# Expert rows gathered by number, results added in memory by accumulating DMAs, expert weights split inside the batch loop

## The chip, the cores and the metric

The kernel runs on one core of one Trainium2 chip. The metric is the device time of one execution in microseconds (us). Before the change three runs gave 1304.9, 1306.76 and 1310.32 us, a median of 1306.76.

The engines: PE (TensorE, the matmuls; PEld is its weight load), DVE (VectorE), ACT (ScalarE), POOL (GpSimd) and SP (SyncE, which here only issues DMAs). ACT and POOL issue DMAs too. POOL alone issues the indirect ones, in which a list of row numbers says which row of a tensor in memory each partition reads or writes. Every engine takes its instructions in order; a wait in front of one holds back all that stand behind it on that engine.

## What is computed

x is (16, 256, 512): 16 batches of 256 tokens of width 512. Cut to what matters:

```
x2   = x + tanh(g_xattn) * mlstm(layernorm(x), ctx, ctx)          # 8 heads of 64, causal decay matrix
n    = layernorm(x2)                                              # 4096 tokens x 512
top2 = top_k(softmax(n @ router_w.T), 2); w = top2 / sum(top2)    # of 16 experts
y    = sum over the 2 chosen experts e of  w_e * (silu(n @ gate_e) * (n @ up_e)) @ down_e    # 512 -> 256 -> 512
s    = (silu(n @ shared_gate) * (n @ shared_up)) @ shared_down    # 512 -> 512 -> 512
out  = x2 + tanh(g_ffn) * (y + s)
```

Each token goes to two experts, so 8192 rows are routed. An expert's weights are 128 partitions x 3072 numbers (1.5 MB). To keep fp32 accuracy each matmul of the second half is done in three parts, with a high and a low part of weights and activations (hi*hi, hi*lo, lo*hi); the weights are therefore "split" into a high part (a cast) and a low part (the rest), 3 MB together.

## The kernel before

**Batch loop.** 16 batches in a software pipeline: step t runs the front of batch t+1 (transposes of x and context, gate rows), the attention of batch t (eight `head`s), the first part of the feed-forward of batch t-1 (layer norm `post_norm` L1353 to L1356, transposes, `router`, shared parts 0 and 1) and the rest of batch t-2 (shared parts 2 and 3, `shared_down`, `rank`). Each engine has this order written out by hand in its own `step`; semaphores tie them together. POOL's `scatter` (L495) writes each normalized row twice, by four indirect DMAs a batch (L501), to `routed_x`, sorted by expert. DVE keeps base rows (x2 + shared part) of all 16 batches in `base_out`, and the routing in `all_hot`, `all_slot`, `all_w`. The shared weights are split at the start by two long POOL instructions (L527, L530) and fill the whole of `w_ring`, which later holds two experts.

**Between.** After the last batch (`drain`) DVE makes tables: how many rows each expert has, where each tile of 128 rows starts, which expert it belongs to. The rest of each expert's last tile is filled with zero rows (`pad_rows`; 17 writes of 256 KB). Expert 0 is split by ACT (L817) and DVE (L1597), expert 1 by POOL (L601, L604).

**Expert stage.** 80 tiles of 128 rows. SP loads tile t (L394, 256 KB) into a ring of four. PE transposes it (`turn_rows` L1125), ACT and DVE make its high and low part, PE multiplies by gate and up (`gate_up` L1137, 12 matmuls), ACT and DVE make the activation (L826, L1603, L1607), PE transposes it (L1146), DVE makes its parts (L1614, L1616), PE multiplies by down (L1155, 6 matmuls). ACT copies the result out (`copy_y` L832) and stores it to `routed_y` (L837). Meanwhile POOL splits the expert after next (L618, L621) and loads one more (L485). PE's order in a tile is: transposes of tile t+2, activation transposes of tile t, gate and up of t+1, down of t.

**Combine.** When all 80 results are stored, POOL gathers for each of 32 token tiles the two result rows of each token (L641, two indirect DMAs of 256 KB), DVE weights and adds them (L1661, L1666), SP stores 256 KB to the output (L423).

## Time and profile before

| what | us |
|---|---|
| median of three timed runs | 1306.76 (1304.9 to 1310.32) |
| span of the profiled execution, first to last instruction | 1302.3 |
| median less span | 4.5 |
| batch loop and drain, up to the last shared matmul | about 794 |
| first expert matmul (L1137) | at 803.98 |
| last result tile stored (L837 issued) | at 1203.90 |
| combine, from there to the end | 98.4 |

The profiled execution has no time of its own beside its span; the 4.5 us is the distance of the span to the median of the other runs. PE is busy 84% of the span, DVE 64%, POOL 38%, ACT 29%. PE is busy in nine tenths or more of nearly every slice from 65 to 715 us and from 830 to 1200 us. In the views, times are from the start of the span; a share in square brackets at a line's end is the idle time before an instruction and what ended it.

### The profile page before, as it was taken

How to read it: one execution, taken by the hardware profiler on the slowest of the kernel's cores; microseconds unless marked ns; L12 is line 12 of the kernel's file. 1: busy time of each engine (PE TensorE's matmuls, PEld its weight loads, DVE VectorE, ACT ScalarE, POOL GpSimd, SP SyncE). 2: the span in 40 equal slices, each digit the busy share in tenths (PEclk: the TensorE clock that was granted, in tenths of full speed). 3: DMA queues.
4: the chain of work that ended last, by engine and by line, in shares of the span. 5: the costliest groups of instructions: out<-in, count | busy, mean ns of one | idle time of the engine just before them, and what ended most of it. 6: DMA issues, size and time to landing. Idle time of an engine off the chain costs nothing.

```text
span 1302.3 us, 24291 instructions
## 1 busy us (share of the span) xinstructions
PE 1098.4 (84%) x6611; PEld 910.9 (70%) x6612; DVE 827.1 (64%) x2212; ACT 371.4 (29%) x820; POOL 491.8 (38%) x368
## 2 busy tenths in 40 slices
PE   2289999999999999999999765999999999999000
PEld 1167888878788887788788664788888888887000
DVE  3756878888788788788877644544444444444455
ACT  1133233424333333343333102223233232232000
POOL 3600222222222222222212335356656566700775
PEclk9666999999999999999999778999999999999555
DMA  5000001110111011001000244555464645321787
GB/s 205 32 33 33 33 34 66 57 42 32 65 57 41 33 65 65 17 32 49 33 1 34 82 172 156 175 181 176 158 205 149 209 151 187 128 98 64 239 283 260
DMA packets 57869, 134.53 MB, mean 103 GB/s; under 512 B 7088, under 2 KB 7088, under 8 KB 57808
## 3 DMA queue, kind: packets, MB, share of 16 engines
q0 software_dynamic: 17472, 59.78, 14.0%
q1 hardware_dynamic: 26128, 48.51, 11.2%
q10 hardware_dynamic: 14208, 25.57, 5.5%
q8 instruction: 22, 0.36, 0.1%
q14 instruction: 39, 0.32, 0.1%
HBM read 83.23 MB, written 50.59 MB: 103 GB/s over the span
## 4 chain that ended last, share of the span: by engine, by line
PE 72%; DVE 12%; issue 7%; DMA 5%; ACT 2%; POOL 0%; DVEq 0%; ACTq 0%; POOLq 0%
PE bank L1137 18%; PE bank L1001 10%; PE bank L1155 9%; PE bank L1012 7%; PE bank L937 5%; PE bank L913 5%; DMA area<-routed_y,y_at 4%; PE bank L879 3%; PE bank L1125 3%; PE bank L942 2%; PE bank L954 2%; PE bank L939 2%; PE bank L955 2%; PE bank L957 2%; PE bank L1146 1%
## 5 line engine op out<-in xcount | busy, mean ns | idle before, releaser
L1137 PE MATMUL bank<-w_ring,x2nT 128*128 x960 | 246.0, 405 | 8.6 <-DVE w_ring L1597 8.6
L1137 PEld LDWEIGHTS bank<-w_ring,x2nT 128*128 128x128 f32 x960 | 175.3, 189 | 48.9 <-issue 10.0
L1001 PE MATMUL bank<-x2nT,w_ring 128*128 128x256 f32 x1536 | 200.2, 288 | 7.8 <-DVE sh_act L1434 7.8
L1001 PEld LDWEIGHTS bank<-x2nT,w_ring 128*128 128x128 f32 x1536 | 190.2, 194 | 9.2 <-DVE sh_act L1434 5.4
L501 POOL DMA_INDIRECT routed_x<-x2n,slot_u x64 | 67.5, 1054 | 192.9 <-DVE slot_u L1424 178.3
L1288 DVE SCALAR_TENSOR_TENSOR area<-bank,area 128x384 f32<-128x384 f32 x128 | 71.4, 557 | 96.7 <-ACT area L712 61.4
L1155 PE MATMUL bank<-w_ring,sh_actT 128*128 x480 | 125.2, 396 | 2.1 <-DVE sh_actT L1616 2.1
L1603 DVE SCALAR_TENSOR_TENSOR ctxT<-ctxT,bank 128x256 f32<-128x256 f32 x80 | 33.7, 421 | 142.7 <-ACT ctxT L826 142.7
L710 ACT ACTIVATE area<-bank,key_log 128x256 f32<-128x256 f32 x128 | 60.7, 474 | 212.1 <-PE bank L944 176.2
L522 POOL TENSOR_TENSOR sh_actT<-sh_act,sh_actT 128x256 fp32r<-128x256 f32 x64 | 54.5, 852 | 167.9 <-ACT sh_actT L727 167.8
L618 POOL TENSOR_TENSOR w_ring<-area,one 128x3072 fp32r<-128x3072 f32 x14 | 74.3, 5304 | 114.4 <-PE bank L1155 114.4
L1155 PEld LDWEIGHTS bank<-w_ring,sh_actT 128*128 128x128 f32 x480 | 90.0, 188 | 24.4 <-issue 2.8
L1012 PE MATMUL bank<-w_ring,sh_actT 128*128 128x512 f32 x384 | 102.5, 412 | 2.3 <-DVE sh_act L1434 1.4
L641 POOL DMA_INDIRECT area<-routed_y,y_at x64 | 67.4, 1053 | 87.1 <-DMA routed_y<-cs_in 67.9
L621 POOL TENSOR_TENSOR w_ring<-area,w_ring 128x3072 fp32r<-128x3072 f32 x14 | 95.6, 6831 | 2.5 <-POOL w_ring L618 2.5
L937 PE MATMUL bank<-area,ctxT 64*128 64x256 f32 x256 | 94.7, 452 | 1.8 <-issue 1.5
L826 ACT ACTIVATE ctxT<-bank 128x256 f32<-128x256 f32 x80 | 30.8, 384 | 204.6 <-PE bank L1137 204.6
L1012 PEld LDWEIGHTS bank<-w_ring,sh_actT 128*128 128x128 f32 x384 | 70.4, 193 | 22.0 <-POOL sh_actT L522 5.4
L1614 DVE CAST sh_actT<-bank 128x256 fp32r<-128x256 f32 x80 | 34.0, 425 | 63.6 <-PE bank L1146 63.3
L832 ACT COPY cs_in<-bank 128x512 f32<-128x512 f32 x80 | 46.9, 587 | 87.2 <-PE bank L1155 87.2
L939 PEld LDWEIGHTS bank<-area,ctxT 64*128 64x128 f32 x256 | 51.1, 200 | 8.8
L937 PEld LDWEIGHTS bank<-area,ctxT 64*128 64x128 f32 x256 | 39.9, 195 | 23.5 <-issue 15.7
(203 smaller groups left out, 2059.0 us busy)
## 6 DMA issues: line engine op xcount, KB each, us to landing
x2n<-routed_x SPq DMA_DIRECT2D x80, 256.0 KB, 2.8
routed_y<-cs_in ACTq DMA_DIRECT2D x80, 256.0 KB, 2.1
base_out<-in_x_dram SPq DMA_DIRECT2D x16, 512.0 KB, 4.4
cs_in<-in_ctx_dram SPq DMA_DIRECT2D x16, 512.0 KB, 3.7
area<-n_L_ffn_expert_gate_dram POOLq DMA_DIRECT2D x16, 512.0 KB, 4.1
area<-in_L_ffn_expert_up_dram POOLq DMA_DIRECT2D x16, 512.0 KB, 4.9
area<-n_L_ffn_expert_down_dram POOLq DMA_DIRECT2D x16, 512.0 KB, 6.9
out_dram<-area SPq DMA_DIRECT2D x32, 256.0 KB, 4.2
```

What stands on the lines that cost most here:

```text
L501: pool.indirect_dma_start(out=routed_x, in_=x2n[:, b.par, j, :], in_offset=None, out_offset=bass.IndirectOffsetOnAxis(ap=slot_u[:, b.par, ...
L618: g.tensor_tensor(w_ring[:, k, 0, :], stage[k], one[:, :].to_broadcast([P, EW]), ALU.mult).then_inc(expert_hi_in.sem, 1)
L621: g.tensor_tensor(w_ring[:, k, 1, :], stage[k], w_ring[:, k, 0, :], ALU.subtract).then_inc(expert_in.sem, 1)
L641: pool.indirect_dma_start(out=y_in[k][:, c, :], in_=routed_y, out_offset=None, in_offset=bass.IndirectOffsetOnAxis(ap=y_at[:, k, c:c + 1], ...
L913: last = mm(SM[0:FG + NH, 0:S], gate_wT[:, c, :], src, start=(c == 0), stop=(c == 2 * DC - 1))
L937: mm(QK[k][:, 0:S], ctxT[rows, b.par, c, 0:P], xnT[rows, b.par, c, 0:S], start=True, stop=True)
L939: mm(QK[k][:, S:TRI], ctxT[rows, b.par, c, P:S], xnT[rows, b.par, c, P:S], start=True, stop=True).then_inc(qk_made.sem, 1)
L1001: last = mm(GU[m][:, at:at + S], w[:, w_part, c, m * P:(m + 1) * P], x2nT[:, x_part, c, :], start=(c + p == 0), stop=(c == DC - 1 and p == 2))
L1012: last = mm(FF[:, :], sh_actT[:, x_part, m, j * P:(j + 1) * P], sh_down[:, w_part, m, :], start=(m + p == 0), stop=(m == SC - 1 and p == 2))
L1137: last = mm(bank[2 + t.par][:, :], xtT[:, x_part, t.par, c * P:(c + 1) * P], w_gu[:, bass.ds(slot, 1), w_part, c, :].rearrange("p a i -> p ...
L1155: last = mm(bank[5 + t.par][:, :], act_aT[:, x_part, t.par, c * P:(c + 1) * P], w_dn[:, bass.ds(slot, 1), w_part, c, :].rearrange("p a i - ...
L1288: v.scalar_tensor_tensor(cmat[:, k, :], QK[k][:, 0:TRI], QK_SCALE, decay[:, k, :], ALU.mult, ALU.mult).then_inc(c_made.sem, 1)
```

## The change

- **Rows go by number.** The normalized rows are stored once, in token order, to `normed` (SP, 512 KB a batch). What is scattered by expert is 8 bytes a row, token number and weight (`meta` to `routed`), still four indirect DMAs a batch. In the expert stage ACT loads the 128 pairs of tile t+4 (`load_meta`, a register load from a table and a DMA), and POOL gathers the tile's rows from `normed` by number.
- **Results are added in memory.** The base rows are stored to `total` (SP, 512 KB a batch). `copy_y` multiplies by the weight, and POOL adds the tile's 128 rows to `total` by an indirect DMA that accumulates (`scatter_y`). It waits for the accumulation of the tile before (`y_added`). ACT waits for the one of tile t-4 before it goes on to `load_meta` and `tanh_gate` of tile t+1. Then eight DMAs of 1 MB, from memory to memory, copy `total` to the output. The combine is gone.
- **Experts are split early.** In step t of the batch loop expert t+1 (in the last, expert 0) is split in six pieces of 128x512: SP loads a piece, ACT casts the high part, POOL subtracts for the low part, SP stores both to `split_w` (512 KB). In the expert stage SP loads one whole split expert (3 MB) by one DMA into a ring of three.
- The split of the shared weights is six POOL instructions of 2048 columns in place of two of 6144. PE's instructions are the same ones in the same order.

The diff, cut to its core:

```
-RING = 2
+RING = 3
 @block.sync
+            def next_piece(t, k, e, e_next):
+                sp.wait_ge(piece_lo.sem, piece_lo.upto(t.n, k + 1))
+                if e is not None:
+                    sp.dma_start(split_w[...piece k of e...], split[:, :, k * PIECE:(k + 1) * PIECE].bitcast(F32)
+                                 ).then_inc(piece_out[k].sem, 16)
+                if k < RAW:
+                    load_piece(e_next if e is None else e, k + RAW)
+                elif e_next is not None:
+                    load_piece(e_next, k - RAW)
...
+            load_expert(1)
+            load_expert(2)
+            told(1)
+            for e in range(3, E):
+                used = sp.value_load(first_tab[0:1, e - 2:e - 1], min_val=0, max_val=TILES)
+                sp.wait_ge(y_made.sem, used + y_made.start)
+                load_expert(e)
+                told(e - 1)
+            told(E - 1)
+            sp.wait_ge(y_added.sem, y_added.upto(TILES - 1))
+            for k in range(HALVES):
+                sp.dma_start(out_tok[k * COPY:(k + 1) * COPY, :], total[k * COPY:(k + 1) * COPY, :]
+                             ).then_inc(copied[0].sem, 16)
 @block.gpsimd
+            def piece(t, k):
+                pool.wait_ge(piece_hi.sem, piece_hi.upto(t.n, k + 1))
+                g.tensor_tensor(split[:, 1, at], raw[:, k % RAW, :], split[:, 0, at], ALU.subtract
+                                ).then_inc(piece_lo.sem, 1)
...
+            def gather(t):
+                pool.wait_ge(meta_in[t.eight].sem, meta_in[t.eight].upto(t.lap8))
+                pool.wait_ge(xt_turned.sem, xt_turned.upto(t.n - XRING))
+                pool.indirect_dma_start(out=xt[:, t.four, :], in_=normed, in_offset=tile_meta[:, t.eight, 0:1])
+            def scatter_y(t):
+                pool.wait_ge(y_copied.sem, y_copied.upto(t.n))
+                pool.wait_ge(y_added.sem, y_added.upto(t.n - 1))
+                pool.indirect_dma_start(out=total, in_=y_out[:, t.four, :], out_offset=tile_meta[:, t.eight, 0:1],
+                                        compute_op=ALU.add).then_inc(y_added.sem, 16)
...
 @block.scalar
+            def piece(t, k):
+                act.wait_ge(raw_in[k % RAW].sem, raw_in[k % RAW].upto(t.n * 2 + k // RAW))
+                act.wait_ge(piece_out[k].sem, piece_out[k].upto(t.n - 1))
+                s.copy(split[:, 0, k * PIECE:(k + 1) * PIECE], raw[:, k % RAW, :]).then_inc(piece_hi.sem, 1)
...
             def copy_y(t):
                 act.wait_ge(y_made.sem, y_made.upto(t.n))
-                s.copy(y_out[:, t.par, :], bank[5 + t.par][:, :]).then_inc(y_copied.sem, 1)
+                s.activation(y_out[:, t.four, :], bank[5 + t.par][:, :], ACT.Copy,
+                             scale=tile_meta[:, t.eight, 1:2]).then_inc(y_copied.sem, 1)
+            def expert_step(t, fill=False, ahead4=True, ahead2=True, ahead1=True):
                 if ahead2:
                     copy_x(t + 2)
+                if not fill:
+                    act.wait_ge(y_added.sem, y_added.upto(t.n - YRING))
+                if ahead4:
+                    load_meta(t + XRING)
                 if ahead1:
                     tanh_gate(t + 1)
                 copy_y(t)
 @block.vector
-            v.tensor_tensor(w_ring[:, 0, 1, :], stage[0], w_ring[:, 0, 0, :], ALU.subtract
-                            ).then_inc(expert_in.sem, 1)
...
-            then(v.tensor_tensor(hot_shift, hot, shift[:, :].unsqueeze(1).to_broadcast([P, B * ST * TOPK, E]),
-                                 ALU.mult))
-            then(v.tensor_reduce(y_slot_f[:, :], hot_shift, AX_X, ALU.add))
```

Where POOL stands at the end of a step of the batch loop, before. The names: `area<-cs_in` copies the values of the next batch, the indirect DMAs are `scatter`, the last row is `keep` of shared part 0:

```order
L508 TENSOR_TENSOR x_rstd<-x_var,minus_half 128x2
L489 ISA
L491 COPY area<-cs_in 128x16x64
L501 DMA routed_x<-x2n,slot_u 67712x512 x4
L520 ISA
L522 TENSOR_TENSOR sh_actT<-sh_act,sh_actT 128x256
```

and now (`w_ring<-raw,w_ring` is the subtraction of a piece):

```order
L616 TENSOR_TENSOR x_rstd<-x_var,minus_half 128x2
L595 ISA
L597 COPY area<-cs_in 128x16x64
L652 REGISTER_ALU
L655 TENSOR_TENSOR w_ring<-raw,w_ring 128x512
L604 ISA
L609 DMA routed<-meta,slot_u 67712x2 x4
L652 REGISTER_ALU
L655 TENSOR_TENSOR w_ring<-raw,w_ring 128x512
L628 ISA
L630 TENSOR_TENSOR sh_actT<-sh_act,sh_actT 128x256
L652 REGISTER_ALU
```

Three of a step's six subtractions (pieces 3, 4 and 5) stand in this part: behind the copy of the values, behind the scatters and behind `keep`.

ACT in the same part of a step, before: the exponentials of head 5 and 6 (`area<-bank`), each with a copy of the transposed rows behind it (`x2nT<-bank`):

```order
L710 ACTIVATE area<-bank,key_log 128x256
L712 ACTIVATE area<-bank,key_log 128x128
L688 ISA
L676 CAST x2nT<-bank 128x4x128
L707 REGISTER_ALU
L710 ACTIVATE area<-bank,key_log 128x256
L712 ACTIVATE area<-bank,key_log 128x128
L688 REGISTER_ALU
L676 CAST x2nT<-bank 128x4x128
```

and now:

```order
L828 ACTIVATE area<-bank,key_log 128x256
L830 ACTIVATE area<-bank,key_log 128x128
L856 CAST w_ring<-raw 128x512
L806 ISA
L794 CAST x2nT<-bank 128x4x128
L825 REGISTER_ALU
L828 ACTIVATE area<-bank,key_log 128x256
L830 ACTIVATE area<-bank,key_log 128x128
L856 CAST w_ring<-raw 128x512
```

The cast of a piece now stands between the exponentials and the copy that PE's next transposes wait for.

POOL in the expert stage, before, one of the experts of a lap (a load of its table entry, the two halves of the split, the loads of a later expert):

```order
L613 TENSOR_LOAD first_tab
L613 ISA x2
L614 REGISTER_ALU
L618 TENSOR_TENSOR w_ring<-area,one 128x3072
L621 TENSOR_TENSOR w_ring<-area,w_ring 128x3072
L485 ISA
L485 DMA area<-in_L_ffn_expert_gate_dram 128x4x256
L485 DMA area<-in_L_ffn_expert_up_dram 128x4x256
L485 DMA area<-in_L_ffn_expert_down_dram 128x2x512
```

and now, two tiles (`x2n<-normed` gathers the rows of a tile, `total<-cs_in` adds its results):

```order
L731 REGISTER_ALU
L733 DMA x2n<-normed,tile_meta 128x512
L743 ISA
L745 DMA total<-cs_in,tile_meta 4224x512
L731 REGISTER_ALU
L733 DMA x2n<-normed,tile_meta 128x512
L743 ISA
L745 DMA total<-cs_in,tile_meta 4224x512
```

POOL has no arithmetic there any more, and two indirect DMAs a tile: 160 in all, the second of each pair behind the wait for the accumulation before it.

## Rows read from the trace of the kernel before

**Rows 1.** Page, part 2: busy tenths in 40 slices of 32.6 us.
```profile
PE   2289999999999999999999765999999999999000
DMA  5000001110111011001000244555464645321787
```
**Rows 2.** Page, part 4: shares of the chain that ended last.
```profile
PE 72%; DVE 12%; issue 7%; DMA 5%; ACT 2%; POOL 0%; DVEq 0%; ACTq 0%; POOLq 0%
```
**Rows 3.** Windows: PE, PEld, DVE, ACT, POOL busy, PE clock, DMA share, GB/s.
```profile
400.00:440.00 40.00, 39.03 (x278) 32.90 (x278) 31.55 (x97) 14.78 (x35) 10.24 (x11) 1.00 0.15 53
1000.00:1050.00 50.00, 50.00 (x245) 40.84 (x244) 23.39 (x51) 14.60 (x30) 34.12 (x12) 1.00 0.54 173
```
**Rows 4.** Timeline (start, us, instruction), before the first head.
```profile
42.12 13.17 POOL L530 TENSOR_TENSOR w_ring<-base_out,w_ring 128x6144 fp32r<-128x6144 f32 x1
44.59 10.97 DVE L1249 SCALAR_TENSOR_TENSOR f_row<-gates,f_row 8x256 f32<-8x256 f32 x1 [2.28 <-ACT f_row L697]
```
**Rows 5.** Page, part 5: POOL's subtraction for one expert.
```profile
L621 POOL TENSOR_TENSOR w_ring<-area,w_ring 128x3072 fp32r<-128x3072 f32 x14 | 95.6, 6831 | 2.5 <-POOL w_ring L618 2.5
```
**Rows 6.** Timeline, one step of the batch loop and the next step's first scatter.
```profile
421.83 0.58 ACT L676 CAST x2nT<-bank 128x512 fp32r<-128x512 f32 x1
422.50 0.68 DVE L1440 TENSOR_TENSOR x2nT<-bank,x2nT 128x512 fp32r<-128x512 f32 x1
423.30 0.61 PE L879 MATMUL bank<-ident,x2n 128*128 128x128 f32 x4
427.35 1.06 POOL L501 DMA_INDIRECT routed_x<-x2n,slot_u  x1 [11.84 <-DVE slot_u L1424]
431.25 1.39 POOL L501 DMA_INDIRECT routed_x<-x2n,slot_u  x1 [0.30 <-issue]
435.30 0.28 PE L925 MATMUL bank<-ident,key_max_rest 40*128 40x40 f32 x2 [0.61 <-issue]
471.03 1.06 POOL L501 DMA_INDIRECT routed_x<-x2n,slot_u  x1 [11.94 <-DVE slot_u L1424]
```
**Rows 7.** Chain of waits, from the batch loop into the expert stage.
```profile
795.29 7.82 DVE w_ring L1597
803.98 4.60 PE bank L1137 x12
819.56 0.10 DVE shift L1637
823.17 0.44 DVE sh_actT L1614
826.67 2.79 PE bank L1137 x12
```
**Rows 8.** Timeline at the same place, POOL and PE.
```profile
788.09 0.74 POOL L522 TENSOR_TENSOR sh_actT<-sh_act,sh_actT 128x256 fp32r<-128x256 f32 x1 [3.77 <-ACT sh_actT L727]
794.34 1.03 PE L1125 MATMUL bank<-ident,x2n 128*128 128x128 f32 x8
```
**Rows 9.** Chain of waits: gate matmuls of tile 79, last `copy_y`.
```profile
1195.57 2.98 PE bank L1137 x12
1203.21 0.59 ACT cs_in L832
```
**Rows 10.** Line L501 (indirect store): ns to issue; DMA, issue to landing.
```profile
L501 POOL DMA_INDIRECT routed_x<-x2n,slot_u x64: 956/962/1389, 169.8 to 769.7; - x64
DMA to landing us min/median/max: 2.7/2.8/3.9
```
**Rows 11.** Line L641 (indirect gather), issue to landing.
```profile
DMA to landing us min/median/max: 3.4/4.8/5.9
```
**Rows 12.** Line L837 (plain store of 256 KB), issue to landing.
```profile
DMA to landing us min/median/max: 2.0/2.1/7.5
```
**Rows 13.** DMA view: 895 to 925 us (40 slices), then 1206 to 1300 us.
```profile
GB/s 0 0 295 281 123 0 76 311 361 279 268 104 161 396 415 415 366 240 90 14 0 79 298 240 82 0 0 0 227 232 240 0 49 164 426 361 350 238 224 410
...
DMA packets 9585, 24.92 MB, mean 265 GB/s; under 512 B 1520, under 2 KB 1520, under 8 KB 9584
```

More of the change, by code:

```diff
@@ L76, in __add__, with __init__ @@
         return Item(self.i, self.offset + k)
+class Tile:
+    def __init__(self, i, offset):
+        self.i, self.offset = i, offset
+        self.n = i * 8 + offset
+        self.half = i * 4 + offset // 2
+        self.lap4 = i * 2 + offset // 4
+        self.lap8 = i + offset // 8
+        self.par, self.four, self.eight = offset % 2, offset % 4, offset % 8
+    def __add__(self, k):
+        return Tile(self.i, self.offset + k)
 def flamingo_kernel(nc, x, ctx_in, g_xattn, g_ffn, igate_w, igate_b, fgate_w, fgate_b, ln_scale,
@@ new lines, in step @@
+            def step(t, more=True, x_more=True, pieces=True, first=False, last=False, route=True, rest=True):
+                C, G, H = t + 3, t + -1, t + -2
+                e = None if last else t.n + 1
+                e_next = None if last else (0 if first == "end" else t.n + 2)
+                if pieces:
+                    for k in range(3):
+                        next_piece(t, k, e, 0 if last else e_next)
+                if more:
+                    sp.wait_ge(ctxT_made.sem, ctxT_made.upto(t.n + 1))
+                    apart(sp)
+                    sp.wait_ge(v_made.sem, v_made.upto(t.n + 1))
+                    apart(sp)
+                    load_ctx(C)
+                if x_more:
+                    sp.wait_ge(x_in[C.par].sem, x_in[C.par].upto(C.half - 1))
+                    apart(sp)
+                    if not isinstance(C.n, int) or C.n >= BASE:
+                        sp.wait_ge(base_stored[C.par].sem, base_stored[C.par].upto(C.half - BASE // 2))
+                        apart(sp)
+                    load_x(C)
+                if pieces:
+                    next_piece(t, 3, e, e_next)
+                if route:
+                    store_normed(G)
+                if pieces:
+                    next_piece(t, 4, e, e_next)
+                if rest:
+                    store_base(H)
+                if pieces:
+                    next_piece(t, 5, e, e_next)
@@ L399, in _ @@
-            with sp.Fori(0, E // 2) as e:
-                row = sp.value_load(pad_tab[0:1, bass.ds(e, 1)], min_val=0, max_val=DUMP - P)
-                sp.dma_start(routed_x[bass.ds(row, P), :], zeros[:, :]).then_inc(padded.sem, 16)
-            sp.dma_start(routed_x[DUMP:DUMP + P, :], zeros[:, :]).then_inc(padded.sem, 16)
+            for k in range(RAW):
+                load_piece(1, k)
+            step(Item(0, -1), x_more=False, pieces=False, route=False, rest=False)
+            step(Item(0, 0), x_more=False, route=False, rest=False)
@@ new lines, in _ @@
+            sp.wait_ge(shared_in.sem, shared_in.upto(2))
+            step(Item(0, 1), rest=False)
+            for n in range(2, 5):
+                step(Item(0, n))
+            with sp.Fori(0, (B - 8) // 2) as i:
+                for u in range(2):
+                    step(Item(i, 5 + u))
+            step(Item(0, B - 3), more=False, x_more=False)
+            step(Item(0, B - 2), more=False, x_more=False, first="end")
+            step(Item(0, B - 1), more=False, x_more=False, last=True)
@@ new lines, in scatter_y @@
+            def scatter_y(t):
+                pool.wait_ge(y_copied.sem, y_copied.upto(t.n))
+                apart(pool)
+                if not (isinstance(t.n, int) and t.n < 1):
+                    pool.wait_ge(y_added.sem, y_added.upto(t.n - 1))
+                    apart(pool)
+                pool.indirect_dma_start(
+                    out=total, in_=y_out[:, t.four, :], in_offset=None,
+                    out_offset=bass.IndirectOffsetOnAxis(ap=tile_meta[:, t.eight, 0:1].bitcast(U32), axis=0),
+                    compute_op=ALU.add,
+                ).then_inc(y_added.sem, 16)
@@ L654, in _ @@
+            for n in range(TILES - 8, TILES):
+                if n + XRING < TILES:
+                    gather(Tile(0, n + XRING))
+                scatter_y(Tile(0, n))
         @block.scalar
```

404 lines of the change are left out of this document (200 added, 204 removed).

## The prediction

> **What bounds the kernel now.** I read the 40 slices first [rows 1]. PE is full in two stretches, and in neither does DMA matter much (0 to 6 tenths). At the end there are three slices in which PE does nothing while the DMA engines are busy at 7 to 8 tenths: the combine. Between the stretches PE dips for three slices. The chain of waits says the same: 72% of it is PE, 12% DVE, 5% DMA [rows 2]. The windows give the slack of the others [rows 3]. In 40 us of the batch loop PE works 39.03, DVE 31.55, ACT 14.78, POOL 10.24; in 50 us of the expert stage PE works all 50, DVE and ACT under half, and the DMA engines are busy 0.54 of the time. So a step of the batch loop (43.7 us, from one batch's scatter to the next [rows 6]) and a tile each cost what PE needs, and a change there can only cost. A tile takes (1195.57 - 826.67) / 76 = 4.85 us, from the gate matmuls of tile 3 to those of tile 79 [rows 7, 9].
>
> What can be won is the combine and the passage from the batch loop to the experts. The question is what the new work does to the two full stretches.
>
> **Tail: -60.** Before, the last result is in SBUF at 1203.8 [rows 9] and the span ends at 1302.3, so 98.5 us. All of that goes. In its place: the last accumulation (4.2, see below), 0.5 for the issue, and 8.39 MB copied from memory to memory. No row shows such a copy. The combine moved 24.92 MB at 265 GB/s in the mean, rows of 2 KB read and written [rows 13]; at that rate 8.39 MB take 31.7 us. The best slice shows 426 GB/s [rows 13]: 19.7 us. If reading and writing memory shared the 265, it would be 63 us. I take 31.7, the nearest row (the mix of reads and writes is the same), and 2.0 for landing as in a plain store [rows 12]. Sum 38.4, gain 60.1. Bounds: 26 to 70, so a gain of 72 to 29.
>
> **Passage: -11.** The last shared matmul and the first transposes end at 795.4; then PE waits for DVE to split expert 0 (7.82 us) and starts at 803.98 [rows 7, 8]. Now expert 0 is split in the last step of the loop. What is late next is the first tile: POOL's gathers stand behind its last `keep`, which ends at 788.83 [rows 8]. The first, issued at 788.9, lands 3.4 later [rows 11] at 792.3, the second 1.3 behind, both before 794.3. Then cast and subtraction of the transposed tile, and PE starts at about 796.4: 7.6 us earlier. The number pairs come before that, at about 785, since the pads are 1 KB each and not 256 KB. Second, DVE no longer computes where each result row lies (L1637 to L1645, 819.56 to 823.17), for which PE waited: 3.6 us [rows 7]. Sum 11.2. If the gathers come late by one landing under load the gain is 7; it can't be above 13. The split of the shared weights has the same columns on POOL, and I cost its six parts at nothing: DVE's row chain now waits for four short instructions in turn where it waited once for 10.97 us [rows 4]; either way it is free when POOL is done. Bounds -4 to +3.
>
> **Batch loop: +20.** Each step gets six casts on ACT (0.58 each, the cast of 128x512 in [rows 6]), six subtractions on POOL (6.831 / 6 = 1.14 each [rows 5]) and about 20 DMA issues on SP, which has nothing else to do (two loads a step before). Stores and loads of pieces are 4.5 MB a step over 43.7 us, or 100 GB/s on engines that are busy 0.15 of the time [rows 3]: hidden, each load has some 10 us before its cast. The sums of ACT (14.8 + 3.5) and POOL (10.2 + 6.8) fit too. What isn't hidden is where they stand. (a) DVE stalls while POOL reads two tensors: an instruction of 8x256 that takes 0.41 us took 10.97 beside POOL's long one, until that ended [rows 4]. Piece 4 follows the scatters, whose last issue ends at 432.64, just when DVE makes the rows on which the logits and then PE's L925 wait; PE already stands 0.61 there [rows 6]. So one subtraction, 1.1 us, falls on the path. (b) The cast of piece 4 stands between the exponentials of head 5 and the copy of the transposed rows. The low part is ready at 423.18, PE uses it at 423.30 [rows 6]: of 0.58 some 0.45 falls on the path. The other pieces meet an idle ACT or have more than 1 us of slack. 1.55 a step, times 13 full steps: 20. Low bound 0 (DVE has 8 us idle in 40). High bound: half of all subtractions on the path, 3.5 a step: 46.
>
> The Trainium skill, "SBUF — State Buffer", section "SBUF: two separate sides", has it that the port pair of VectorE and GpSimd is an exclusive lock for the whole instruction, against DVE operations with two SBUF inputs or in a 2-port mode. By that rule each of the six pieces can stall DVE by up to its full length, and the step could lose 6.8 us where DVE is the last to be ready; the trace's 10.97 us agrees with the lock, and its DVE idle time speaks for less.
>
> **Expert stage: +31.** The tile's own work is unchanged. SP, ACT and DVE stay under half load. Two things are new: a chain of accumulations, each of which waits for the one before, and 3.1 MB an expert in one DMA where 1.5 MB was loaded. Call u the period of the chain on quiet DMA engines. A plain indirect store of 128 rows lands 2.8 after its issue starts, and POOL needs 0.3 to go on [rows 6, 10]: u can't be under 3.1. An accumulation also reads its target. If that read came wholly before the store it would be 3.4 + 2.8 + 0.3 = 6.5 [rows 11]. A gather, which has that read, takes 0.6 more than a store; I add about as much again for the doubled bytes and the longer descriptor list: u = 4.2, nearer to the lower row. The gather of another tile (1.25 of issue) lies in the flight of an accumulation. On top, a transfer that meets a loaded engine takes up to 7.5 for 2.1, that is 5.4 more [rows 12], and 3.1 MB at 350 to 426 GB/s [rows 13] occupy the engines for 8 us, so each expert's load meets one accumulation. With 80 / 16 = 5 tiles an expert: chain 5 x 4.2 + 5.4 = 26.4, PE 5 x 4.85 = 24.3. The chain is longer by 2.1, and ACT's wait for tile t-4 hands this on: behind it stand `load_meta`, `tanh_gate` and with it PE's down. The four buffers take up a burst, not a mean. 15 experts with loads: 31. Bounds: 0 (u = 3.1), and 15 x (37.9 - 24.3) = 204 (u = 6.5).
>
> **Sum.** 1302.3 - 60 - 11 + 20 + 31 = 1282; with the 4.5 by which the median stands over the span, 1287.
>
> On the accumulation the Trainium skill, "Collectives: The Full Stack", section "The bandwidth ceiling: the fold count and why AG ≠ RS ≠ AR", says that an add in the DMA engine costs no time of its own but a second read on the same ring. By that rule u would be a store and the doubled bytes; 256 KB at 426 GB/s are 0.6 us, so u = 3.7 and the sum 1256 (rival 1). No row of this case shows an accumulation.
>
> **Rivals.**
> 1. *The chain is hidden.* The second read costs only its bytes, u = 3.7 or less: 5 x 3.7 + 5.4 = 23.9, under PE's 24.3. For it: of a store's 2.8 only 0.96 is issue [rows 10], the rest can hold a read beside it; and 4.8 was the median of gathers on engines at eight tenths [rows 1, 11]. Against it: read, then write of memory is a path that neither has. Time: 1287 - 31 = 1256.
> 2. *The chain decides the stage, and the kernel is slower.* One mechanism: u at 5.5, because the target is read, added and written one after the other. Then 5 x 5.5 + 5.4 = 32.9 an expert, 8.6 over PE, 129 in all: 1287 + 98 = 1385. It turns the sign when the stage loses over 51, which is 3.4 an expert, from u = 4.5 on. For it: 4.5 is only 0.3 above my value, and the wait is strictly serial. Against it: only the upper bound of the rows reaches that far.
> 3. *The batch loop pays.* Pieces stop DVE or ACT on PE's path at 3.5 us a step: +46 in place of +20, 1313, no change. For it: DVE is at eight tenths there [rows 3]. Against: ACT and POOL have over half their time free.
>
> **How the numbers follow.** Forecast 0.37 (own range 1265 to 1302), rival 1 0.27, rival 2 0.27, rival 3 0.09. The likeliest is 1287. 0.5% of the median is 6.5 us, about what can be told from no change: 1300.2 to 1313.3 is "same". Faster: nearly all of the forecast and all of rival 1, less what a slow copy takes, 0.58. Slower: rival 2 from u = 4.54 and the bad half of rival 3, 0.32. Same: 0.10. The range reaches down to rival 1 with a quicker copy (1256 - 12, and a part of the batch loop's 20): 1240; up to rival 2: 1385. Where signs differ this much, the forecast's own 1265 to 1302 says more.
>
> **What would show it.** Steps: PE's last wait before the first gate matmul is for the tile, not for DVE, at about 816 (796 + 20). Batch steps are 45.2 us apart, L925's wait grows from 0.6 to about 1.7. Accumulations land about 4 us after issue, about 9 when an expert is loading; ACT waits for y_added in some tiles of each expert. A tile takes 5.2 in the mean. The copy takes 32. I am wrong if tiles stay at 4.85 (rival 1), if POOL waits for the accumulation before every tile and tiles take over 5.5 (rival 2), or if steps are 47 us or more (rival 3).

## The result: slower by 11%, and the profile after

Before 1308.54 us (1304.9 to 1310.51), after 1447.71 us (1445.75 to 1448.41). The ratio is 1.1065 with a 95% interval of 1.1035 to 1.1095. The forecast was 1287, its range ended at 1385: wrong in sign and out of range. The profiled execution after has a span of 1444.1 us against 1302.3, so 141.8 more, and it divides into the four terms of the sum without a rest:

| stretch, in the two traces | predicted | measured |
|---|---|---|
| batch loop (to the end of the last shared matmul: 794.34 to 847.86) | +20 | +53.5 |
| passage (from there to the first gate matmul: 9.64 to 2.15) | -7.6 | -7.5 |
| expert stage (first gate matmul to the moment at which the last result can go out: 399.8 to 560.1) | +31 - 3.6 | +160.3 |
| tail (98.5 to 34.0) | -60 | -64.5 |

Before, the last result can go out when it is in SBUF, at 1203.8. After, it is there at 1403.4 but has to wait until the accumulation of tile 78 has landed, at 1410.1.

The page after, part 2: busy tenths of PE, granted clock of PE, and DMA, in 40 slices of 36.1 us.

```profile
PE   3389999999999999999999576777777777779870
PEclk9568999999999999999999798888999999989995
DMA  5243453444444353434331166666666666765548
```

The three idle slices of [rows 1] are one now. But from slice 24 to 36 PE is mostly at seven tenths where it had nine. Its clock, 1.00 in [rows 3], is below full in both long stretches (0.93 and 0.90 in the windows below). Part 4 of the page, the chain that ended last, against [rows 2]:

```profile
PE 39%; DMA 33%; issue 11%; DVE 11%; ACT 2%; ACTq 1%; POOLq 0%; DVEq 0%; POOL 0%
DMA total<-cs_in,tile_meta 30%; PE bank L1135 9%; PE bank L1146 7%; PE bank L1071 5%; PE bank L1047 4%; PE bank L1076 2%; PE bank L1088 2%; DVE area L1462 2%; PE bank L1073 2%; PE bank L1013 2%; PE bank L1091 2%; PE bank L1089 1%; PE bank L
```

PE had 72% of the chain, now 39%. 30% of the span is one kind of transfer, the accumulation. Windows of the same places as [rows 3], then of the whole stage:

```profile
165.00:650.00 485.00, 458.00 (x3026) 387.40 (x3025) 399.86 (x1081) 193.24 (x435) 200.32 (x185) 0.93 0.44 144
850.00:1410.00 560.00, 431.38 (x1912) 337.88 (x1912) 182.06 (x399) 129.28 (x238) 201.02 (x155) 0.90 0.63 158
```

**The chain of accumulations.** The chain of waits in the middle of the stage (start, length, what):

```profile
1089.40 11.79 DMA total<-cs_in,tile_meta
...
1102.03 4.66 DMA total<-cs_in,tile_meta
...
1107.53 5.03 DMA total<-cs_in,tile_meta
...
1112.60 0.58 issue
...
1113.39 5.07 DMA total<-cs_in,tile_meta
...
1119.30 5.08 DMA total<-cs_in,tile_meta
...
1125.32 11.58 DMA total<-cs_in,tile_meta
```

Start to start the quiet period is 5.3 to 6.1 us nearly always, 5.8 in the mean: 4.6 to 5.1 in flight and 0.8 to 0.9 until POOL starts the next issue. Where a 3 MB load sets out at the same moment it is 12.6 in the mean. That is the arithmetic of the stage. From the start of the first accumulation (867.5) to that of the last (1410.9) there are 79 periods: 66 x 5.76 + 13 x 12.56 = 543.4. (Two of the 15 loads set out before the first accumulation, so 13 meet one. The text of e5_meta has 64 periods of 5.9 and 15 of 12.6; that comes near 560 only because it also leaves out the start.) The other 17.5 us lie between the first gate matmul and the first accumulation, and they hold a wait of the same kind: the small load of tile 4's numbers, issued beside the two first 3 MB loads:

```profile
854.21 11.05 DMA tile_meta<-routed
```

The groups of the accumulation (L745) and of the expert's load (L509), from issue to landing:

```profile
L745 POOL DMA_INDIRECT total<-cs_in,tile_meta x80: 1549/1592/1638, 867.5 to 1410.9; - x80
DMA to landing us min/median/max: 4.5/4.9/13.3
...
DMA to landing us min/median/max: 10.6/11.1/18.9
```

An accumulation takes 1.59 us to issue against 0.96 of the plain indirect store [rows 10], and lands after 4.9 against 2.8.

**The batch loop.** Timeline of the end of one step (start, length, instruction, idle time before):

```profile
549.95 1.88 DVE L1400 CAST max_parts<-max_row 8x256 bf16<-8x256 f32 x1
550.37 1.30 POOL L655 TENSOR_TENSOR w_ring<-raw,w_ring 128x512 fp32r<-128x512 f32 x1
554.40 0.29 PE L1059 MATMUL bank<-ident,key_max_rest 40*128 40x40 f32 x2 [2.09 <-issue]
557.62 5.13 PE L1135 MATMUL bank<-x2nT,w_ring 128*128 128x256 f32 x24
```

DVE's cast (8x256, 0.28 us at the shortest in this trace) stands until POOL's subtraction of piece 4 is over, and PE's wait, 0.61 in [rows 6], is 2.09. The prediction had both. What it did not have is the last row: the 24 shared matmuls, which take 3.05 us elsewhere in the step, take 5.13. The windows around it show the clock:

```profile
552.00:558.00 6.00, 3.81 (x21) 3.00 (x20) 4.46 (x16) 0.93 (x4) 1.94 (x2) 0.78 0.63 218
558.00:564.00 6.00, 6.00 (x34) 5.68 (x34) 2.85 (x8) 1.90 (x5) 2.70 (x3) 0.65 0.55 186
564.00:570.00 6.00, 6.00 (x52) 5.68 (x51) 5.16 (x11) 3.20 (x8) 3.33 (x3) 1.00 0.49 157
```

After the wait of 2 us the granted clock is at its lower level, 1.2 GHz, for 6.8 us (555.4 to 562.2), and then back at 2.4. In the trace of before, with a wait of 0.6 at this place, it stays at full from 215 to 640 us. Here it falls ten times in that stretch: seven times behind this wait of 2.1 us (six of them for about 7 us, one for 3.5), and three times (at 357, 402 and 637) behind two waits of 0.28 and 0.31 us that stand 13 us earlier in a step (twice for 7 us, once for 3.5). Those two stand there in all ten steps; in the three steps in which a fall follows them, the wait at L1059 is 0.3 to 0.6. The step is longer by 4.1 us; first scatters of two batches nine steps apart give (640.07 - 217.80) / 9 = 46.9, before it was (641.45 - 213.45) / 10 = 42.8:

```profile
217.80 1.05 POOL L609 DMA_INDIRECT routed<-meta,slot_u  x1 [11.25 <-DVE slot_u L1561]
640.07 1.05 POOL L609 DMA_INDIRECT routed<-meta,slot_u  x1 [11.26 <-DVE slot_u L1561]
```

### The profile page after: what moved, and what is told of

Its sections match the earlier page's. It is cut to its first block, busy times and chain, and to the rows that moved or that the text cites. A ratio compares the mean times of both kernels' runs of the same rounds, so it can differ in the third digit from the quotient of the medians.

```text
span 1444.1 us, 24782 instructions
## 1 busy us (share of the span) xinstructions
PE 1170.5 (81%) x6611; PEld 957.7 (66%) x6612; DVE 823.0 (57%) x2109; ACT 429.7 (30%) x915; POOL 552.5 (38%) x489
## 4 chain that ended last, share of the span: by engine, by line
PE 39%; DMA 33%; issue 11%; DVE 11%; ACT 2%; ACTq 1%; POOLq 0%; DVEq 0%; POOL 0%
DMA total<-cs_in,tile_meta 30%; PE bank L1135 9%; PE bank L1146 7%; PE bank L1071 5%; PE bank L1047 4%; PE bank L1076 2%; PE bank L1088 2%; DVE area L1462 2%; PE bank L1073 2%; PE bank L1013 2%; PE bank L1091 2%; PE bank L1089 1%; PE bank L1114 1%; DMA tile_meta<-routed 1%; DMA x2n<-normed,tile_meta 1%
## 5 line engine op out<-in xcount | busy, mean ns | idle before, releaser
L1271 PE MATMUL bank<-w_ring,x2nT 128*128 x960 | 264.0, 428 | 1.3 <-issue 1.3
L745 POOL DMA_INDIRECT total<-cs_in,tile_meta x80 | 127.3, 1591 | 320.4 <-DMA tile_meta<-routed 174.7
L1135 PE MATMUL bank<-x2nT,w_ring 128*128 128x256 f32 x1536 | 216.9, 303 | 4.5 <-DVE sh_act L1569 4.5
L1135 PEld LDWEIGHTS bank<-x2nT,w_ring 128*128 128x128 f32 x1536 | 207.7, 211 | 5.3 <-issue 3.8
L655 POOL TENSOR_TENSOR w_ring<-raw,w_ring 128x512 fp32r<-128x512 f32 x96 | 135.7, 1413 | 67.7 <-ACT w_ring L856 67.3
L1259 PE MATMUL bank<-ident,x2n 128*128 128x128 f32 x320 | 57.6, 309 | 119.0 <-DMA x2n<-normed,tile_meta 118.7
L609 POOL DMA_INDIRECT routed<-meta,slot_u x64 | 66.9, 1045 | 184.0 <-DVE slot_u L1561 158.0
L1259 PEld LDWEIGHTS bank<-ident,x2n 128*128 128x128 f32 x320 | 39.2, 154 | 147.5 <-DMA x2n<-normed,tile_meta 145.0
L733 POOL DMA_INDIRECT x2n<-normed,tile_meta x80 | 79.2, 990 | 43.4 <-issue 22.0
L952 ACT CAST x2nT<-bank 128x512 fp32r<-128x512 f32 x80 | 46.7, 585 | 130.8 <-PE bank L1259 130.6
## 6 DMA issues: line engine op xcount, KB each, us to landing
w_ring<-split_w SPq DMA_DIRECT2D x15, 3072.0 KB, 11.1
```

The source lines that it names most:

```text
L609: pool.indirect_dma_start(out=routed, in_=meta[:, b.par, c, :], in_offset=None, out_offset=bass.IndirectOffsetOnAxis(ap=slot_u[:, b.par, c ...
L655: g.tensor_tensor(split[:, 1, at], raw[:, k % RAW, :], split[:, 0, at], ALU.subtract).then_inc(piece_lo.sem, 1)
L733: pool.indirect_dma_start(out=xt[:, t.four, :], in_=normed, out_offset=None, in_offset=bass.IndirectOffsetOnAxis(ap=tile_meta[:, t.eight, ...
L745: pool.indirect_dma_start(out=total, in_=y_out[:, t.four, :], in_offset=None, out_offset=bass.IndirectOffsetOnAxis(ap=tile_meta[:, t.eight ...
L1135: last = mm(GU[m][:, at:at + S], w[:, w_part, c, m * P:(m + 1) * P], x2nT[:, x_part, c, :], start=(c + p == 0), stop=(c == DC - 1 and p == 2))
L1259: last = tr(bank[t.par][:, c * P:(c + 1) * P], xt[:, k, c * P:(c + 1) * P], ident[:, :])
```

## The experiments

Totals are medians of four runs; e2, e3, e5, e6, e11, e13 and e14 ran once. "Stage" is first gate matmul to the start of the last accumulation: 560.9 us in the changed kernel. It repeats well: four kernels in which it is unchanged (e4, e11, e13, e14) have 560.7 to 562.6. The batch loop repeats less well. In the six traces in which it is unchanged (after, e1, e2, e3, e5, e6) the first gate matmul comes at 850.0 to 858.5 and a step takes 46.9 to 47.4 us; in the six in which only piece 4 has moved (e4, e7 to e10, e12) it is 822.2 to 826.5 and 44.7 to 45.0. A difference of 0.3 us a step or of 8 us at the first gate matmul between two single traces therefore shows nothing.

**First four: which cost is it?**

```
e1_back2   -  pool.wait_ge(y_added.sem, y_added.upto(t.n - 1))
           +  pool.wait_ge(y_added[t.par].sem, y_added[t.par].upto(t.half - 1))     # one event for each parity
e2_plain   -  compute_op=ALU.add,
e3_noload  -  load_expert(e)                                                       # for e >= 3
e4_p4late     if route: keep(G, 0)     # POOL's step: this now stands ahead of
              if attend: piece(A, 4)   # this
```

> Change: an accumulation waits for the one two tiles back instead of the one just before (two in flight; the last eight tiles keep the old wait). Theory A (the serial wait sets the stage: in the changed kernel 5.9 us from one accumulation to the next, 12.6 where one meets a weight load): the chain of accumulations leaves the critical path, a tile costs 4.9 to 5.4 us as in the kernel before, the stage from first gate matmul to last landing falls from 560 to about 400 to 440 us, the total to about 1290 to 1330. Rival B (bandwidth: accumulations, gathers and 3 MB loads slow each other, the wait only shows it): two in flight take nearly twice as long each, the stage stays above 500 us and the total above 1390.

Measured 1421.58 us, ratio to before 1.0876 (1.0847 to 1.0906). The stage is 532 us, only 29 less. It is rival B's figure, but not B's cause: the accumulations' share of the chain falls from 30% to 2%, and what stands there instead, once per expert, is the 1 KB load of a tile's numbers, or in four cases a gather. The chain of this kernel:

```profile
1055.00 1.42 PE bank L1295 x6
1056.44 0.48 ACT cs_in L971
...
1057.72 12.62 DMA tile_meta<-routed
...
1071.31 3.45 DMA x2n<-normed,tile_meta
```

The end of an expert releases at one moment SP's 3 MB load and ACT's small load; the small one takes 11.7 to 13.4 us (least 1.7, median 2.6), POOL's gather stands behind it, and PE has only two tiles in hand. Theory A was half of the truth: the serial wait was the limit, but a second one stood close behind it.

> Change: the same indirect DMAs with the same waits, but they store instead of adding (the results of the second expert overwrite those of the first, so the output is not the reference's). Theory A1 (what is long in the chain is the adding: issue 1.6 us and 4.9 us to landing against 0.96 and about 3 of the plain indirect DMAs in the batch loop): the period falls from 5.9 to about 4.0 us, below the 4.85 that the engines need for a tile, the stage to 400 to 450 us, the total to about 1290 to 1340. Rival A2 (the length is that of any 256 KB scatter over 128 rows of 2 KB): period still above 5.3, total above 1400.

Measured 1406.68 us. The stores land after 2.7 us in the median (the line's row: 2.7/2.7/10.5) against 4.9, and their issue takes 0.98 against 1.59. So adding in memory costs 2.2 us of latency and 0.6 of issue here; A1 is right on the piece. On the total the figure is rival A2's (above 1400), for the same reason as in e1: the chain has a small load of 9.8 to 12.1 us for nearly every expert, and the stage is still 514.8.

> Change: the 3 MB loads of experts 3 to 15 are left out (the matmuls use the weights that lie there, so the output is not the reference's). Theory A: 15 meetings of an accumulation with a load cost some 6.7 us each; 13 of them go, the stage falls from 560 to about 470 us, the total by 85 to about 1360. Rival B (the quiet period alone sets the stage, meetings are made up for later): total falls by less than 30.

Measured 1369.47 us, 78 less; the stage is 478. The 13 collisions cost 6.4 us each (83 / 13), as theory A has it (6.8 by the two periods, 12.56 - 5.76). What is left is the bare chain. Its line, and a part of its chain:

```profile
DMA to landing us min/median/max: 4.7/4.9/5.8
...
1061.36 4.90 DMA total<-cs_in,tile_meta
1066.30 0.58 issue
...
1067.10 4.99 DMA total<-cs_in,tile_meta
1072.13 0.58 issue
```

5.8 us a period, longer than the tile's 4.85, with no load at all. No accumulation takes over 5.8 us without a load beside it.

> Change: in a step of the batch loop GpSimd's subtraction of piece 4 stands behind the shared expert's first subtraction instead of right behind the scatters, away from VectorE's chain of row operations. Theory C (that subtraction stalls the row chain by 1.4 us, TensorE waits 2.1 us and its clock is then half for 6.8 us, in every step): the wait falls under 1 us, the dips of the clock in the loop vanish, a step takes 43 to 44.5 instead of 46.8 us, the total falls by 30 to 50 us to about 1400 to 1417. Rival D (the ScalarE casts and the transfers of the pieces make the step longer): the step stays above 46 us, the total within 10 us of 1447.

Measured 1425.22 us, ratio to before 1.0916 (1.0895 to 1.0936). The first gate matmul comes at 824.6 instead of 850.0 and the stage is the same (560.7): all 25 us are the batch loop's, the step is 44.9. The wait at this place (L1058 there) is 0.7 us at most between 215 and 640 us, and no dip follows it. But the theory's "the dips vanish" is wrong, and step and total miss its ranges (43 to 44.5, 1400 to 1417): behind the two waits 13 us earlier in a step, which stand in the changed kernel too, a dip of 3.5 to 7 us follows in five of nine steps. The timeline of one, and the window from there:

```profile
436.11 0.63 PE L1012 MATMUL bank<-ident,x2n 128*128 128x128 f32 x4 [0.28 <-issue]
437.05 0.17 PE L1100 MATMUL bank<-chosen,before_b 128*128 128x16 bf16 x1 [0.31 <-DVE gates L1373]
```

```profile
437.00:443.00 6.00, 5.95 (x29) 5.32 (x30) 3.35 (x12) 2.62 (x6) 2.03 (x3) 0.54 0.01 2
```

Before, the second wait (0.30) stood alone and the clock stayed. Here ACT's cast of piece 4 adds 0.28 just ahead of it, the term (b) of the prediction, and the lower level follows from 437.6 to 444.4. The dip here is one of the long ones. So theory C is right for 2.0 of the 4.1 us of a step. In every second step the loop jumps back; behind two of these four jumps (at 282 and 462 us) a second dip follows:

```profile
457.72 0.56 DVE L1421 SCALAR_TENSOR_TENSOR area<-bank,area 128x384 f32<-128x384 f32 x1 [3.74 <-issue]
458.51 0.43 PE L1087 MATMUL bank<-area 128*128 128x65 f32 x2 [1.46 <-DVE area L1421]
460.99 4.62 PE L1134 MATMUL bank<-x2nT,w_ring 128*128 128x256 f32 x24 [1.16 <-DVE sh_act L1568]
```

**Next four: undo the causes together.**

```
e5_meta     META = 16; load_meta(t + 8) in place of load_meta(t + 4); the loops of ACT and POOL run over 16 tiles
e6_paced    for k in range(6):              # one 512 KB DMA each
                sp.wait_ge(expert_dma[g % 2].sem, expert_dma[g % 2].upto(g // 2 - 1))     # g = (e - 1) * 6 + k
                sp.dma_start(...[:, at], ...[:, at]).then_inc(expert_dma[g % 2].sem, 16)
e7_three    e1_back2 + e5_meta + e4_p4late
e8_three_paced   e7_three + e6_paced
```

> Change: the 1 KB loads of a tile's numbers and weights are issued 8 tiles ahead instead of 4 (16 places in the ring instead of 8); the accumulations keep their wait for the one before. Theory A (in the changed kernel the chain of accumulations alone sets the stage: 64 periods of 5.9 and 15 of 12.6 us is 567, the stage is 560): total within 20 us of 1447. Rival E (GpSimd stands 10 to 12 us behind a small load that was issued together with a 3 MB load, and that sets the stage, as the chain of e1_back2 shows with 12.2 to 12.7 us per expert): the stage falls by 15 times 5 to 7 us, the total to about 1350 to 1375.

Measured 1450.16 us, stage 559.5: no change, as theory A has it. While each accumulation waits for the one before, the small load is hidden behind that chain.

> Change: an expert's 3 MB are loaded by six DMAs of 512 KB, at most two under way at a time, instead of by one. Theory F (a small transfer waits because the whole 3 MB lie queued ahead of it on the same 16 engines): no accumulation and no small load takes over about 8 us any more (now 11 to 13), 15 long ones become some 45 with 2 to 3.5 us more each, the total falls by 20 to 60 us. Rival G (bytes count, not their place in the queue): the same 7 us per expert are lost in smaller portions, total within 15 us of 1447 or above.

Measured 1423.67 us, stage 530: theory F. The longest piece of the chain in the whole stage is 8.6 us instead of 13.3.

> Change: three together: accumulations wait for the one two tiles back, the small loads go 8 tiles ahead, and piece 4 stands behind the shared subtraction in the batch loop. Theory (both the serial wait and the late small load had to go, and e1_back2 took away only the first): the tile comes back to 4.9 to 5.2 us as in the kernel before, stage 395 to 420, batch loop as in e4_p4late (first gate at about 828 us), tail 34: total 1260 to 1290, faster than the kernel before by 1 to 3%. Rival (the engines are held by transfers as such): stage over 450, total over 1320.

Measured 1345.33 us, ratio 1.029 (1.025 to 1.0331): 102 less than the changed kernel, but short of the 1260 to 1290; stage (484.4) and total are the rival's (over 450, over 1320). Against e1_back2 the stage is 48 us shorter: that is what the early small load is worth now, which alone was worth nothing. The chain shows the next in line, the gather:

```profile
1055.27 0.70 ACT cs_in L970
...
1057.08 1.59 POOL total L749
1058.67 0.30 issue
1058.97 9.69 DMA x2n<-normed,tile_meta
1068.71 1.12 PE bank L1264 x4
```

It stands behind an accumulation on POOL, so it is issued when the last expert's last result is ready, together with the 3 MB load, and takes 9.1 to 12.4 us.

> Change: e7_three with the expert's load in six paced DMAs as in e6_paced. Theory: with two accumulations in flight and the small loads early, a 12 us landing is covered already, so pacing changes the total by less than 8 us against e7_three. Rival: the gathers (4 tiles ahead, 3.3 to 12 us) still stop TensorE at each load in e7_three and pacing takes 20 us or more off.

Measured 1282.7 us, ratio to before 0.9823 (0.9793 to 0.9853): 63 less than e7_three, not under 8. The rival of the expectation is right; the gathers in the chain now take 6.3 to 7.4 us, and the stage is 419.4.

**Last of the stage and the tail.**

```
e9_gather          e8_three_paced + gather(t + 5) in place of gather(t + 4), ahead of scatter_y(t)
e10_gather_whole   e7_three + the same
e12_direct         e9_gather, total = out_tok;
                   + compute_op=ALU.add, bounds_check=T - 1, oob_is_err=False
                   - the eight sp/act.dma_start(out_tok[...], total[...])
```

> Change: e8_three_paced with the gathers one tile further ahead on GpSimd (the gather of tile t+5 ahead of the accumulation of t; the buffer is free by then). Theory: what is left in e8's chain (per expert a gather that lands after 6.3 to 7.4 us and holds TensorE 1 to 2 us, the tile at 5.17 us on average) goes, a tile costs 4.9 us, total 15 to 25 us under e8's 1282.7. Rival: in e8 the 16 DMA engines are full (230 to 290 GB/s in the stage), and an earlier gather only comes later elsewhere: within 6 us of e8.

Measured 1267.3 us, ratio 0.9669 (0.9629 to 0.971), 15 less than e8_three_paced, stage 406.4. PE is full again, with DMA busy 0.89 of the time at 231 GB/s; a tile takes 4.9 us. Below it the same window of e10_gather_whole:

```profile
850.00:1200.00 350.00, 350.00 (x1707) 285.62 (x1706) 162.63 (x357) 110.00 (x213) 181.73 (x142) 1.00 0.89 231
```

```profile
850.00:1200.00 350.00, 335.45 (x1626) 272.04 (x1625) 154.84 (x339) 105.73 (x203) 176.61 (x137) 1.00 0.85 219
```

The rival (a full DMA only moves the wait) fell.

> Change: e7_three (3 MB in one DMA) with the gathers one tile further ahead. Theory: in e7_three TensorE waits 5 to 6 us once per expert for a gather that was issued together with a 3 MB load (9.7 to 11.5 us to landing); 4.9 us more lead cover that, 15 times 5 us go: total 1345 to 1262-1280, so pacing is then worth under 10 us. Rival: accumulations of 11 to 13 us, two in flight, then hold ScalarE's result buffers and TensorE instead: total stays above 1310.

Measured 1286.49 us, ratio 0.9837 (0.9787 to 0.9887): 59 less than e7_three by two lines. It misses the range by 7 us, and pacing is still worth 19: with whole loads PE stands once per expert or two behind a gather of 11 to 13 us. The rival's accumulations (9 to 13 us) are in the chain too, with 7% of the span, though the total is below its 1310.

> Change: e9_gather with the base written to the output itself and the accumulations made there; the padding rows' numbers lie beyond its 4096 rows and are skipped, and the last copy goes. Theory: the copy's 31 us and its issue and landing go (the tail is then the last accumulation, some 5 us): total about 30 us under e9_gather. Rival: accumulating in the output's memory or skipping rows costs more per accumulation: less than 15 us under e9_gather.

Measured 1230.08 us, ratio to before 0.9404 (0.9363 to 0.9445): 37 less than e9_gather, somewhat more than the theory's 30. From the start of the last accumulation to the end are 5.2 us. It is the fastest. Part 4 of its page, PE has the chain back as in [rows 2]:

```profile
PE 74%; DVE 13%; issue 7%; ACT 2%; DMA 2%; DVEq 0%; ACTq 0%; POOLq 0%; POOL 0%; SPq 0%
```

A reservation: with two accumulations under way, two neighbouring tiles must not add to the same row. Here they don't: the tokens of an expert stand in order and each expert has several tiles. With another router nothing in these kernels would ensure it.

**What else the pieces cost the loop.**

```
e11_short_sub    g.tensor_tensor(split[:, 1, at], ...)    # at: 8 of the 512 columns, after the first step
e13_short_cast   e11_short_sub + s.copy(split[:, 0, ...], ...) on 8 of the 512 columns
e14_short_load   e13_short_cast + the loads of the pieces 8 columns wide
```

> Change: the changed kernel with GpSimd's subtractions of the pieces cut from 512 to 8 columns after the first step (the low halves of the experts' weights are then wrong; ScalarE's casts, all transfers and all waits stay). Theory C (GpSimd's long subtractions beside VectorE make the loop longer): a step takes 43 to 44 instead of 46.8 us, first gate matmul at 805 to 815 instead of 850, total 1405 to 1412. Rival D (casts and transfers): the step stays above 45.5 us, total above 1430.

Measured 1419.19 us; first gate matmul at 821.4, step (661.68 - 214.82) / 10 = 44.7. Between the two theories: all six subtractions together cost no more, within the spread of the traces, than the one that e4_p4late had moved.

> Change: e11_short_sub with ScalarE's casts of the pieces cut from 512 to 8 columns too (all transfers and waits stay; the weights are wrong). Theory H (the casts, 0.6 us each on ScalarE between the heads' exponentials, make what is left): the step falls from 44.7 to 42.8-43.3 us, first gate matmul from 821 to 798-806, total near 1399. Rival I (transfers or the longer instruction stream): the step stays above 44.2.

Measured 1414.34 us; first gate at 818.7, step 44.5. Theory H fell: 0.2 us a step less is within the spread. The wait of 0.28 is gone and with it the dip behind it. What is left in the two steps from 430 us on is one dip behind the jump, from 455.7 to 459.0. Of the ten steps from 216 us on, four have neither a jump nor a dip and take 42.3 us; two have no jump but a dip and take 43.9; the four with a jump, behind which the clock falls each time, take 46 to 48. In the trace of before they are 42.1 to 42.2 without a jump and 43.7 to 44.0 with one. So with all transfers running, but short casts and subtractions, a step that has neither jump nor dip is as short as before to 0.2 us.

> Change: e13_short_cast with the loads of the pieces cut from 512 to 8 columns (the stores of 512 KB per piece stay). Theory H: no further change, the step within 0.3 us of e13. Rival I: the step falls by 0.7 us or more against e13.

Measured 1401.1 us; first gate at 804.4, step 43.5. Rival I: without the loads a step is 0.9 us shorter and the first gate comes 14 us earlier, more than the spread of the traces, though each kernel ran once. It is the steps with a jump that gain: they fall to 44.4 to 46.3 us, the others stay at 42.3, or 43.8 with a dip. DVE's idle time in front of its first long instruction at the jump is 2.7 to 3.0 us in the trace of before, 2.7 to 4.1 in the changed kernel, 2.9 to 4.0 in e4_p4late, 3.6 to 4.4 in e13_short_cast and 3.3 to 3.8 in e14_short_load. The cause of the longer ones isn't shown: a fetch of its instructions held up by the transfers would do it, but no run loaded the queue without the pieces or took the jump away.

In all these kernels the granted clock still falls at least once in most pairs of steps. Its means over windows of 90 us (from 215 to 665 us) are below the 1.00 of before: 0.92 to 0.96 in the changed kernel, 0.94 to 0.98 in e4, 0.94 to 0.97 in e11, 0.96 to 0.98 in e13, 0.97 to 1.00 in e14. An estimate from these rows: the step's length times the share missing from the full clock is 3.4, 1.6, 2.0, 1.2 and 0.7 us, and the steps stand 4.1, 2.1, 1.9, 1.7 and 0.7 us above the 42.8 of before. So the clock could account for most of what remains. Why the same wait is followed by a dip in some steps and not in others stays open: one of 0.7 us at the same place by none in e4, but by one within 3 us three times in e14 (the waits at 262.7, 436.3 and 481.1).

## Why the prediction was wrong

The step that failed is the expert stage: the period u of the chain of accumulations, put at 4.2 us and measured at 5.8, and the price of a meeting with a load, put at 5.4 and measured at 6.4 to 6.8. With them the chain is longer than PE's work by 11 us an expert and not by 2, so that the stage lost 160 us where 31 were forecast. That the chain would be the limit was forecast; its size, which set the sign, was not.

- **Tail (-60): right.** 64.5. The eight copies are issued from 1415.7 on, and the span ends at 1444.1. The row I took for their rate, 265 GB/s, was near enough; e12_direct shows what was left to win.
- **Passage (-11): right.** 7.5 for the forecast's first half of 7.6; the second half, DVE's 3.6 us, lies in the stage and can't be told apart there. The tile was even there early: PE's transposes follow the shared matmuls at once, and its last idle time, 1.28 us, is that of the cast and the subtraction, not of the gather, as the prediction's signs had it.
- **Batch loop (+20): mis-sized, by 33 us.** Part (a) named the right instruction and the right wait: 1.1 us forecast, 1.5 measured in seven of ten steps, and e4_p4late confirms it. Part (b), the cast, was 0.45; the wait is 0.28, and e13_short_cast removes it. The 43.7 us that I took for a step before is a single one, with a jump in it; the mean of ten is 42.8. What failed is the step from a wait to a time: I added the waits' lengths and no more. A wait of 2.1 us in a full stretch is followed by 6.8 us at half clock, in which PE does, as an estimate, 3.4 us less than at full; the mean clock gives the same 3.4 for a mean step. The rest of the 4.1 is part of the wait. And I cost 100 GB/s of transfers as hidden since each load has time before its cast; in e14_short_load the loads are worth 0.9 us a step. The Trainium skill's rule on the shared port ("SBUF — State Buffer", "SBUF: two separate sides") held in kind: the cast on DVE stood 1.88 us beside the subtraction. But of six subtractions only one lay on the path.
- **Expert stage (+31): the term that turned the sign.** u was 5.8 and not 4.2. 1.0 us of that is the landing (4.9 against 3.9), 0.6 is POOL's way from a landing to the next issue (0.8 to 0.9), which I took from the 0.3 between issues that wait for nothing. The true value lay inside my bounds (3.1 to 6.5), at the end that I had called a whole read before the store, and I chose nearer to the lower row. The collision was 5.4 and measured 6.4 to 6.8. By the prediction's own sum that is 5 x 5.8 + 6.8 = 35.8 an expert against PE's 24.3, so 15 x 11.5 = 172 for a measured 160; the exact count of periods is given above.
- **The rule that adding costs only a second read** (the Trainium skill, "Collectives: The Full Stack", "The bandwidth ceiling: the fold count and why AG ≠ RS ≠ AR") gave u = 3.7 and rival 1. Here e2_plain measures it: 2.7 us to landing without the add, 4.9 with it, for 256 KB in 128 rows. That rule is drawn from the bandwidth of large transfers. I priced the second read by its bytes, 0.6 us; with the add the landing came 2.2 us later and the issue took 0.6 more. Whether the read or the addition takes that time no run separates.
- **Rival 2 is what happened**, with a larger price (u = 5.8 for 5.5), and rival 3's mark, 47 us a step, was as good as reached beside it (46.9). I had held them to be alternatives, and the range ended where one alone ends.
- **What the prediction didn't see at all**: that three small transfers of a tile, accumulation, numbers and gather, are all released at an expert's end, together with its 3 MB. Each takes 10 to 13 us then. The serial wait covered the other two, so that removing it alone (e1_back2) took 29 us off the stage, removing the late load alone (e5_meta) 1, and all of them, with pacing and the earlier gather (e9_gather), 154.

## What to carry to other kernels

Where a chain of DMAs waits one for another, its period is landing plus the whole way back to the next issue, and it must be set against the engine's time per tile with the worst neighbour in it; a large DMA that is released by the same event as small ones should go in pieces with a bounded number under way. In a stretch where TensorE is full, look at the granted clock behind a new wait, even a short one: here one of 2.1 us cost some 3.4 us more than its own length. And when one limit goes, look at the chain again before believing the sum: here four had to go before the time moved to where the first was expected to bring it.

## What the runs showed of the hardware that I had not expected

- An accumulating indirect DMA of 128 rows of 2 KB takes 1.59 us to issue and 4.9 to land, the same without adding 0.98 and 2.7.
- A transfer of 1 KB took up to 13.4 us (e1_back2), a gather of 256 KB up to 13.1 (e10_gather_whole), when issued with one DMA of 3 MB that itself takes 11.1 in the changed kernel and 13.1 in e1_back2. With six DMAs of 512 KB, two under way, none of these took over 8.7. In the first case a small transfer takes as long as the large one.
- With those in order the DMA engines run 350 us at 0.89 busy and 231 GB/s and TensorE loses nothing.
- Each of seven waits of 2.1 us in the changed kernel was followed by 1.2 GHz, six times for about 7 us and once for 3.5; those of 0.6 to 0.7 us at the same place were not in e4_p4late, but within 3 us two of them were in e13_short_cast and three in e14_short_load. Two of 0.28 and 0.31 within 1 us, elsewhere in the step, were in three of ten steps of the changed kernel and in five of nine of e4_p4late. One of 0.3 alone at that place never was.
- Indirect accumulation with rows beyond the bound skipped, straight into the output, costs no more per DMA than into a scratch tensor (e12_direct against e9_gather: 1.59 us to issue in both, 5.9 and 6.2 to land in the median).
